# A new prologue for a cross-attention and ternary-FFN kernel on one core: x and queries ahead of the ternary weights, the second weight's tiles inside the first attention

## The reference

```
q, k, v  from  layernorm(x) @ Wq.T, ctx @ Wk.T, ctx @ Wv.T
w    = softmax(q1 k1.T) - lam * softmax(q2 k2.T)        # 16 heads of 32; two heads share k and v
attn = rmsnorm(w @ v) * g * (1 - LAMBDA_INIT);  x = x + attn @ Wo.T
tern(w) = clip(round(w / mean|w|), -1, 1) * mean|w|     # the mean is over the whole weight
h = layernorm(layernorm(x)) * ln1_g + ln1_b
h = gelu(h @ tern(w1).T + b1)                           # 2048 hidden
h = layernorm(h) * ln2_g + ln2_b
x = x + h @ tern(w2).T + b2
```

## Time and profile before

| | us |
|---|---|
| median of 3 runs (lowest, highest) | 2459.5 (2456.2, 2461.03) |
| the profiled execution | 2460.22 |
| its span | 2456.9 |
| TensorE busy | 2301.5 (94%) |
| VectorE busy | 1719.6 (70%) |
| ScalarE busy | 1339.5 (55%) |
| GpSimd busy | 1012.2 (41%) |
| granted TensorE clock, mean | 0.973 |

### The profile page before, as it was taken

How to read it: one execution, slowest core, us unless ns; L and a number is a source line. 1 busy time by engine, 2 the same in 40 slices (tenths; PEclk the granted TensorE clock), 3 DMA queues, 4 the chain that set the end, 5 groups by cost and what they waited for, 6 DMA issues and landing times.

```text
span 2456.9 us, 35564 instructions
## 1 busy us (share of the span) xinstructions
PE 2301.5 (94%) x13663; PEld 1082.5 (44%) x13663; DVE 1719.6 (70%) x2714; ACT 1339.5 (55%) x1943; POOL 1012.2 (41%) x823
## 2 busy tenths in 40 slices
PE   8488999999999999999999999999999999999978
PEld 5243444535344453535444353534445353544433
DVE  3865858678585868768586776858586785857563
ACT  3325555546555555556555555655555465555544
POOL 0220543617153452716345271625436172534517
PEclk9688999999999999999999999999999999999989
DMA  6220203021130302111030202103030211202000
GB/s 256 74 77 11 69 15 89 13 69 26 37 84 15 90 15 68 25 60 44 23 97 15 78 15 69 36 23 82 15 101 19 65 27 33 72 15 74 15 22 17
DMA packets 105643, 125.85 MB, mean 51 GB/s; under 512 B 22496, under 2 KB 74268, under 8 KB 104964
## 3 DMA queue, kind: packets, MB, share of 16 engines
q1 hardware_dynamic: 105476, 123.60, 17.4%
HBM read 51.80 MB, written 20.36 MB: 29 GB/s over the span
## 4 chain that ended last, share of the span: by engine, by line
PE 69%; DVE 19%; issue 3%; ACT 3%; POOL 3%; DMA 2%; SPq 1%; POOLq 0%; ACTq 0%; DVEq 0%
PE ps L1325 16%; PE ps L1337 9%; PE ps L1347 7%; PE ps L1272 5%; PE ps L1225 5%; PE ps L1250 4%; PE ps L1173 4%; PE ps L1279 4%; PE ps L1174 3%; PE ps L1175 3%; DVE attn_raw L928 2%; DVE arena L987 2%; DVE arena L876 2%; DVE arena L890 2%; PE ps L1255 2%
## 5 line engine op out<-in xcount | busy, mean ns | idle before, releaser
L526 POOL TENSOR_TENSOR attn_raw<-attn_raw 128x512 f32<-128x512 f32 x448 | 580.2, 1314 | 146.5 <-ACT attn_raw L685 138.7
L1325 PE MATMUL ps<-rows,w1T 128*128 128x512 f16 x2048 | 485.5, 380 | 24.1 <-DVE rows L982 24.1
L890 DVE TENSOR_REDUCE arena<-ps 128x3 f32<-128x462 f32 (+1 forms) x704 | 413.8, 619 | 96.5 <-PE ps L1225 95.4
L494 POOL TENSOR_TENSOR q<-q 128x512 f16<-128x512 f32 x128 | 155.9, 1222 | 695.3 <-ACT q L631 678.5
L680 ACT ACTIVATE attn_raw<-ps,vec_cols,wstep 128x512 f32<-128x512 f32 x256 | 198.6, 776 | 267.0 <-PE ps L1325 265.2
L987 DVE SCALAR_TENSOR_TENSOR arena<-attn_raw,vec_cols,arena 128x512 f16<-128x512 f32 x256 | 233.1, 911 | 84.7 <-ACT arena L683 83.2
L1325 PEld LDWEIGHTS ps<-rows,w1T 128*128 128x128 f16 x2048 | 191.0, 97 | 220.7 <-DVE rows L982 37.2
L651 ACT ACTIVATE arena<-ps 128x1024 f32<-128x1024 f32 x128 | 131.6, 1028 | 266.6 <-PE ps L1250 266.6
L1347 PE MATMUL ps<-w2T,arena 128*128 128x512 f16 x1088 | 271.1, 379 | 0.0
L910 DVE SCALAR_TENSOR_TENSOR p<-arena,p 128x512 f16<-128x512 f32 x128 | 88.1, 689 | 254.4 <-ACT p L655 254.4
L1225 PE MATMUL ps<-k_att,stack_raw 96*128 96x154 f16 x2048 | 223.2, 234 | 23.1 <-DVE arena L890 21.6
(11 more groups left out here) (164 smaller groups left out, 3436.5 us busy)
## 6 DMA issues: line engine op xcount, KB each, us to landing
stack_raw<-q SPq DMA_DIRECT2D x768, 64.0 KB, 2.0
arena<-in_x SPq DMA_DIRECT2D x16, 1024.0 KB, 6.2
arena<-in_x SPq DMA_DIRECT2D x64, 256.0 KB, 2.6
out<-arena SPq DMA_DIRECT2D x64, 256.0 KB, 2.0
arena<-in_L_ffn_w SPq DMA_DIRECT2D x8, 1024.0 KB, 10.5
stack_raw<-in_L_xattn_Wq SPq DMA_DIRECT2D x8, 256.0 KB, 10.8
k_att<-k_store SPq DMA_DIRECT2D x4, 490.0 KB
k_store<-attn_raw SPq DMA_DIRECT2D x12, 160.0 KB
```

The source lines that it names most:

```text
L526: ins = pool.tensor_tensor(acc[:, e, :], acc[:, e, :], src[:, j % NG, :], ALU.add)
L890: dve.tensor_reduce(negmax[:, tt, u0:u1], ps[:, row_bank(c, tb), 0:(u1 - u0) * S].rearrange("p (u s) -> p u s", s=S), AX.X, ALU.max, negat ...
L1325: ins = pe.matmul(ps[:, B_H + j % 2, :], w1T[:, k, j * P:(j + 1) * P], rows16[:, e, k, :], start=(k == 0 and e == 0), stop=(k == KD - 1 an ...
```

## The change

1. The x rows of block 0 are loaded right behind the value weights, into the buffer of the f16 rows (`x_in0`), and their statistics and rows are done inside `setup`. Wo is loaded ahead of Wq. Keys start on tile 12, values on tile 16, with four `v_new` buffers in place of two. The weights' sums are cut anew (five pieces of w1, four of w2), and three of the nine come behind setup.
2. The mask difference is no longer subtracted by VectorE or GpSimd: TensorE multiplies one mask by the identity and adds the other times the negative identity, in f32 PSUM, which transposes it too.
3. The prologue's order is one list per engine. Queries stand first, only the 16 tiles of w1 are in it, and the maxima are spread among them. The 16 tiles of w2 (`w` in `FIRST`) are done in block 0's attention, through one PSUM bank; the vectors that need w2 in block 0's hidden layer (`output_vectors`).
4. In blocks 1 to 15 the transposes of the maxima move from the end of the block before behind the first quarter of `ffn_late`.
5. In block 0 SP stacks the first two pairs of queries, then loads `x_res` of block 0 (behind the last ternary product), then `x_in` of block 2.

```diff
-WFIRST = 13
-PROLOGUE = [... t0 to t17, "xs t18 t19 xr t20 t21 xt t22 t23 q0 t24 t25 q1 t26 t27 q2 t28 t29 q3 t30 t31 q4 ys r0 m0 yr q5 m1 q6 q7 yt m2 m3"
+PE_PROLOGUE = tokens("x0 q0 q1 a0 q2 t0 t1 t2 q3 t3 t4 t5 q4 t6 t7 m0 q5 t8 t9 m1 q6 t10 m2 t11 q7 m3 t12 m4 t13 m5 t14 "
+                     "m6 t15 m7 m8 m9 m10 b0 x1 n0")
+DVE_PROLOGUE = tokens("x0 a0 t0 t1 t2 t3 t4 t5 t6 t7 t8 m0 t9 t10 m1 t11 m2 t12 m3 t13 m4 t14 s1 m5 t15 r1 m6 m7 m8 m9 m10 "
+                      "n0 b0 x1 n1")
+FIRST = tokens("q0 w0 s0 w1 s1 w2 v0 w3 s2 w4 v1 w5 s3 w6 v2 w7 s4 w8 a0 v3 w9 s5 w10 v4 q1 s6 a1 v5 q2 s7 q3 w11 v6 w12 a2 w13 "
+               "v7 w14 a3 w15")
...
+                    if n == N_KV_TILES - 1:
+                        load_x_in(0)
...
                 if i + 1 < NBLK:
-                    for p in range(QM // 2):
+                    for p in range(0 if i else QATT // 2, QM // 2):
                         stack_queries(i + 1, p, i)
...
+                if i == 0:
+                    for p in range(QATT // 2):
+                        stack_queries(1, p, 0)
+                    sp.wait_ge(s_ternT, NTERN)
+                    for tt in range(TT):
+                        load_x_res(0, tt)
...
             def ternary(n):
-                pe.wait_ge(s_tern[n % 2], n // 2 + 1)
-                if n >= 2:
-                    pe.wait_ge(s_ternC, n - 1)
+                pe.wait_ge(s_sign, n + 1)
+                if n >= JH:
+                    pe.wait_ge(s_ternC, n)
+                elif n >= 4:
+                    pe.wait_ge(s_ternC, n - 3)
...
                 for k in range(KD):
-                    ins = pe.transpose(ps[:, TERN_BANK[n % 2], 0:TB // 2].bitcast(F16)[:, k * P:(k + 1) * P],
-                                       tern[:, n % 4, k * P:(k + 1) * P], ident16[:])
+                    cols = slice(k * P, (k + 1) * P)
+                    pe.matmul(ps[:, bank, cols], pair[:, 0, cols], ident16[:], start=True, stop=False)
+                    ins = pe.matmul(ps[:, bank, cols], pair[:, 1, cols], nident16[:], start=False, stop=True)
...
                     elif what == "e" and i:
                         ffn_late(i - 1, n, range(JH // 4))
+                        transpose_maxima(i)
...
                 for j in range(JH - FLAG, JH):
                     ffn_step(i, j, banks)
-                if ahead:
-                    transpose_maxima(i + 1)
```

More of the change, by code:

```diff
@@ L296, in build @@
         tiles += [(wv[r * P:(r + 1) * P, :], P, "wv", r) for r in range(VM // P)]
+        tiles += [(wo[r * P:(r + 1) * P, :], P, "wo", r) for r in range(KD)]
         tiles += [(wq[r * P:(r + 1) * P, :], P, "wq", r) for r in range(QM)]
-        tiles += [(wo[r * P:(r + 1) * P, :], P, "wo", r) for r in range(KD)]
         N_KV_TILES = 2 * BATCH + D // P + VM // P
@@ L385, in setup @@
                 load_values(0)
-                load_x_in(1)
-                sp.wait_ge(s_sign, NTERN)
-                for tt in range(TT):
-                    load_x_res(0, tt)
             def load_keys(b):
@@ L530, in iteration @@
                 ahead, ahead2 = i < NBLK - 1, i < NBLK - 2
-                for what, n in ATTEND:
+                for what, n in ATTEND if i else FIRST:
                     if what == "g" and i:
@@ L699, in iteration @@
                         attn_hi(i, n)
+                    elif what == "w":
+                        ternary_copy(JH + n)
                     elif what == "q" and ahead:
@@ L1024, in iteration @@
                 ahead, ahead2 = i < NBLK - 1, i < NBLK - 2
-                for what, n in ATTEND:
+                if i == 0:
+                    for n in range(SIGNS_AHEAD):
+                        ternary(JH + n)
+                for what, n in ATTEND if i else FIRST:
                     if what == "s":
@@ L1031, in iteration @@
                         attn_lo(i, n)
+                    elif what == "w" and n + SIGNS_AHEAD < JH:
+                        ternary(JH + n + SIGNS_AHEAD)
                     elif what == "g" and i:
@@ L1163, in ternary_vectors, with output_vectors @@
                 ins.then_inc(s_bias, 1)
-                pe.wait_ge(s_lncopy, 1)
-                pe.wait_ge(s_pick, 2)
-                for e in range(2):
-                    ins = pe.matmul(ps[:, 1 + e, :], pick[:, e, :], ln2_rows, start=True, stop=True)
-                ins.then_inc(s_spread, 1)
+            def output_vectors(j):
+                if j == VECTORS_AT[1]:
+                    pe.wait_ge(s_ternC, NTERN)
+                    pe.wait_ge(s_l2, 2)
+                    wait(pe, s_q32, 1, QM, QM)
+                    for n in range(JH):
+                        ins = pe.matmul(ps[0:4, 1, :], ln2_16[:, :, :, n].rearrange("p e h -> p (e h)"), w2T[:, n, :],
+                                        start=(n == 0), stop=(n == JH - 1))
+                    ins.then_inc(s_lnrow, 1)
+                elif j == VECTORS_AT[3]:
+                    pe.wait_ge(s_lncopy, 1)
+                    pe.wait_ge(s_pick, 3)
+                    for e in range(2):
+                        ins = pe.matmul(ps[:, e, :], pick[:, e, :], ln2_rows, start=True, stop=True)
+                    ins.then_inc(s_spread, 1)
             def split_product(dst, w_hi, w_lo, r_hi, r_lo, first, last):
@@ L1185, in x_transposes @@
                     wait(pe, s_xhat1, c, TT, tt + 1)
+                    if c == 2 and tt == 0:
+                        pe.wait_ge(s_rows, 2)
+                    rows = (x_in if c else x_in0)[:, tt, :]
                     for k in range(KD):
-                        ins = pe.transpose(ps[:, x_bank(c, tt), k * P:(k + 1) * P], x_in[:, tt, k * P:(k + 1) * P], ident[:])
+                        ins = pe.transpose(ps[:, x_bank(c, tt), k * P:(k + 1) * P], rows[:, k * P:(k + 1) * P], ident[:])
                     ins.then_inc(s_xt, 1)
@@ L1363, in iteration @@
                 ahead, ahead2 = i < NBLK - 1, i < NBLK - 2
-                for what, n in ATTEND:
+                tiles_done = queries_done = 0
+                for what, n in ATTEND if i else FIRST:
                     if what == "s":
                         scores(i, n)
+                    elif what == "w":
+                        if queries_done > 1:
+                            wait(pe, s_q32, 1, QM, queries_done)
+                        ternary(JH + n)
+                        tiles_done = n + 1
                     elif what == "v":
```

399 lines of the change are left out of this document (225 added, 174 removed).

## The result

| | before | after |
|---|---|---|
| median of 4 runs, us | 2460.0 (2456.2 to 2461.0) | 2421.9 (2420.2 to 2424.1) |
| profiled execution, us (span) | 2460.2 (2456.9) | 2423.5 (2421.5) |
| TensorE busy, share of the span | 94% | 94% |
| mean granted clock | 0.973 | 0.983 |

The ratio is 0.9848, with a 95% interval of 0.9831 to 0.9865: 38 us faster. The forecast was 2417 with a range of 2402 to 2433.

The account below looks back on a forecast made before the run. TensorE was taken to bound the blocks, VectorE and DMA round trips the prologue. Terms -41.2 - 3.0 + 7.8 + 3.4 + 5.1 - 15 = -42.9 from 2460.2 gave 2417 us, range 2402 to 2433.

Parts of the forecast that it names:

- Step 1: Setup of the weights: x transposes start at 75 us (70 to 80), counted from VectorE's last weight piece at 82.0 before.
- Steps 2 and 3: Prologue behind setup: first sign at 92 us, first row scores at 104.5, row maxima done at 151 instead of 198.5.
- rival C: Prologue: setup faster (70 us), queries warm, first row scores at 100, less cost in block 0's attention; 2405 us, chance 0.10.
- Step 4: Way into block 0: first scores at 162.5 us instead of 203.66 (-41.2), score group 1 sooner behind them (-3.0).
- Step 5: Sixteen ternary tiles in block 0's attention, through one PSUM bank: +6.9 us there, 0.9 at its end, +7.8 in all.
- Step 6: Behind block 0's attention: x_in(2) is late behind stacked pairs and x_res, VectorE waits 0 to 6 us, taken as +3.4.
- Step 7: Output vectors in block 0's hidden layer: 16 + 4 matmuls, 3.6 and 1.5 us of TensorE, +5.1 us.
- Step 8: Maxima transposed later in 15 blocks: the 1.04 us wait for VectorE is covered, -15 us (10 to 16).
- Rival A: Block 0's attention pays the full hand-over through one bank and x_in the full 6 us: 2428 us, chance 0.16.
- B: Block ends: the later transposes gain only half, 7.5 us, because add_ffn's chain then ends last; 2424 us, chance 0.08.
- D: Block 0's attention: TensorE's granted clock falls to 1.2 GHz through pauses for copies, +54 us; 2471 us, chance 0.02.
- E: Setup: x's 1 MB ahead of the weights ends setup at 95 us, with full hand-over too; about 2450 us, chance 0.04.

Follow-up runs that it names:

- Experiment 2: Three edits of the changed kernel's setup: values' buffers moved (2420.6 us), key stores on ScalarE's queue (2430.7 us), buffers moved plus three weight loads later (2414.1 us).
- e7: Changed kernel without the 16 w2 ternary tiles in block 0's attention, the weight set to zero: 2424.2 us, ratio 0.9859.
- e1: Changed kernel with the four transposes of the split maxima put back at the end of a block: 2437.6 us, ratio 0.9909.
- e12: Kernel before, with only the transposes of the split maxima moved behind the first quarter of ffn_late: 2445.4 us, ratio 0.9950.
- e8: Changed kernel; in blocks 3, 7, 11 x_in loads first, then the first stacked pair, next keys, other pairs, next values last: 2414.7 us, ratio 0.9822.
- e2: Changed kernel with the last two value batches of the setup in the buffers of k_att and v_att: 2420.6 us, ratio 0.9843.
- e3: Changed kernel; in block 0 the load of x_in(2) stands ahead of the four x_res loads: 2422.7 us, ratio 0.9847.
- e5: Changed kernel with the setup's twelve key stores issued by ScalarE's queue instead of SyncE's: 2430.7 us, ratio 0.9885.
- e6: Changed kernel without the output vectors' matmuls and VectorE copies in block 0's hidden layer: 2417.0 us, ratio 0.9835.
- e9: Changed kernel with e2's buffers and three 1 MB loads of the second weight moved behind the last Wq tile: 2414.1 us, ratio 0.9818.
- e4: Changed kernel; in blocks 3, 7 and 11 the load of x_in stands ahead of the next keys' load: 2428.1 us, ratio 0.9875.

## Why the prediction was right, and where it was not

The forecast stood 42.9 us below the profiled execution; the span fell by 35.4. Both parts of the forecast are there, the prologue and the transposes; some of its terms were wrong and made each other good. Step by step:

- **Step 1 (setup), 75 forecast, 82.2 measured: wrong.** "Removed: the wait of 5.8 us for the v_store round trip" is true, but the step went over VectorE's work alone and took the DMA queue for granted, except for the 1 MB of x; 82.2 lies outside its own bounds of 70 to 80. The new homes lie in the buffer of the keys, so VectorE waits for their stores (10.1 us), and the Wq tiles, now behind Wo, stand between these stores in a queue with 9 MB of weights and x in front of them or between. Experiment 2 shows both: 3.7 us for the homes, 6.0 for the three loads ahead; without them 72.5. In neither account is the swapped loop of the values' product, 4 x 2.6 us of TensorE's work. That the order Wo before Wq has its part is read from the two queues and was not tried by itself.
- **Steps 2 and 3: 7.2 us late at their start, 2.5 at their end.** First sign 15.0 us behind the x transposes (17 forecast), since q0 ran at full clock; split maxima 44.3 us behind the first row scores (46.5), since the queries between them did too (q2, ahead of them, ran its first seven matmuls at 1.2 GHz). That was half of rival C.
- **Step 4:** first scores at 163.5 instead of 162.5: the way there from the split maxima took 10.0 us, 11.5 forecast. So the start is right to 1.0 us only because three steps were too long by 6.2 us in all where the first was too short by 7.2; that much is luck. The 3.0 us for q0 being done were there: score group 1 comes 3.07 us behind group 0 instead of 6.21. A part of the 6.21 was the clock: 0.50 from 203.7 to 208.4 us before, 1.00 after.
- **Step 5: its mechanism was too small.** 6.9 us forecast for the tiles, 9.1 measured between the kernels (50.4 instead of 41.3): 5.8 of TensorE's own work and 3.4 of waits. The step had only the one bank and ScalarE's copies in it; of the three waits one is for a tile's copy (1.30), the others are for VectorE's compares (1.20) and a query's copy (0.86). The 0.9 for the end did not come. Leaving the tiles out gives 6.8, which looks like the forecast's 6.9, but e7 had a stretch at a clock of 0.51 of its own. Nor do steps 5 and 6 add up as a sum: of the 6.8 only 2.4 show in block 0's time, since SyncE's stack holds x_in back.
- **Step 6:** 3.4 forecast, 3.3 measured; its fix brought 2.7.
- **Step 7:** 5.1 forecast, 5.7 by leaving them out: the 16 matmuls took 3.6 us as before, the four f32 ones 1.9 and not 1.5.
- **Step 8:** 15 forecast; 0.91 us a block, 13.7 in 15 blocks; by the totals 15 (e1) and 12 to 13 (e12). "0.1 to 0.3 us may stay" held: 0.14 stayed.
- **What no step had:** the waits for x_in behind block 0 (blocks 3, 7, 10 and 11), 10.5 us after against 6.7 before, 3.9 of the 7.5 us missing. e8 shows what those of blocks 3, 7 and 11 come from and that they can go; that of block 10, where no keys are loaded, is not explained. Why the change made them longer is open: 6.7 and 6.6 us in the profiles of before and e12, 7.1 to 10.8 in eight of the changed order (after, e1, e2, e3, e5, e6, e7, e9), with the same issues in SyncE's queue.

The missing 7.5 us: 1.0 in step 4's point, 1.1 in block 0's attention, 0.6 in the vectors, 1.3 in the transposes, 3.9 in x_in, less 0.4 elsewhere. The 40.2 us by which the first scores come earlier are read from the two traces as a whole. No run takes back the order of the prologue, the mask difference on TensorE or the w2 tiles' move out of it, so what each of them brings is not shown.

Rival A (2428) had the full hand-over, +16 in the stretch, which did not come; B (half the transposes' gain) is out by e1 and e12; D is out, since the granted clock was 1.00 over block 0's attention; E had the right place (x ahead of the weights' queue) and far too large a price.

## What to carry to other kernels

A new home for a buffer brings new waits with it: list who used the place before and when its last transfer lands, and put the bytes ahead of each transfer in the same queue into the sum. Where several waits end at one point (tiles and a queue of stacked loads here), leaving one out shows what it is worth there: 2.4 of 6.8 us. Such a run needs its own clock and starting point looked at, or its difference is put down to what was left out. Order a queue by when each transfer is needed, with every reader counted: moving one load ahead (e4) brought nothing, ordering all of them by need (e8) brought 7 us.

## What the runs showed of the chip

- The issue of a DMA can cost far more than its usual 0.4 us: three stores of 160 KB took 6.7 and 6.2 us to issue on SyncE while 377 to 389 GB/s moved, 5.1 and 5.3 at 200 to 240 GB/s, 3.8 to 4.2 with 3 MB less ahead (125 to 228 GB/s), and 2.2 to 13.4 us on ScalarE's queue, whose engine stood still for 13.1 us.
- TensorE did nothing but f32 transposes from 60 to 87 us after: at a granted clock of 0.50 from 70 to 85.5 us (gaps of 0.5 to 2.4 us up to 82.2, then 16 transposes without one), at 1.00 from 86 us on. The query behind them ran at full pace, 0.22 us a matmul; the forecast had taken it cold. After the next 3.3 us of idle time the clock was 0.50 from 96.3 to 99.3 us.
- Short work in a gap went with a clock that stayed up: at the first two score groups of block 0 it was 1.00 after, with a tile in each gap; in e7, without them, it was 0.51 from 170.0 to 173.5 us (1.7 us lost).
- 32 matmuls of 26 columns into four groups of 32 PSUM rows took 1.93 us with the groups taking turns and 4.57 us one group after the other.
- A VectorE instruction of 128x4 (L1066) took 1.00 us beside GpSimd's four additions (305.68 to 310.66), against 0.17 us in the kernel before.
